# Copying half of the transposed attention probabilities with VectorE instead of ScalarE in the last batch of cross attention

## The chip, the cores and the metric

The kernel runs on one core of one Trainium2 chip. The metric is the device time of one execution in microseconds (us). The engines are PE (TensorE), DVE (VectorE), ACT (ScalarE), POOL (GpSimd) and SP (SyncE, which here only issues DMAs). Each has its own instruction stream in program order, and the streams meet only through semaphores.

## What is computed

The kernel is a whole decoder layer on x of shape (8, 256, 512): a gated delta rule, then cross attention, then a quantised feed-forward. The change touches the cross attention alone:

```python
qh = q.reshape(b, s, 4, 4, 32)            # 4 groups of 4 heads, 32 wide
scores = einsum('bghsd,bgtd->bghst', qh, kh) / sqrt(32)
probs = softmax(scores, axis=-1)
out = einsum('bghst,bgtd->bghsd', probs, vh)
return out.reshape(b, s, 512) @ Wc.T + bc
```

There are 8 batches of 256 query tokens and 256 context tokens. Keys and values are the same context tensor. After the attention, x + out is normalised and quantised for the feed-forward, and the feed-forward's weights are quantised beside the attention.

## The kernel before, in words

The function `attend` holds the stage. A batch's 256 queries are two row tiles u = 0 and 1, and the heads are four groups c = 0 to 3. So a batch is 8 slots (c, u), walked by every engine in the order (0,0), (0,1), (1,0), ... (3,1). The last batch is batch 7, `step(B - 1, True, False, False)`. It projects nothing for a later batch, so PE has less to do in it than in the others.

A tile goes through these steps, each by one engine:

- PE `scores` (L1805) writes the scores of 4 heads into two PSUM banks, `ps_s[u][0]` and `ps_s[u][1]`. It waits for both counters `pt0_done[u]` and `pt1_done[u]` of the tile before in the same banks.
- DVE `maxima` (L2115, two reduces) finds the row maxima of both banks.
- ACT `weigh` (L1989) makes 4 exponentials into `probs[u]`, with the row sums beside.
- PE `turn_probs` (L1813, 8 transposes) writes the probabilities, transposed, back into the same two banks. The first bank holds the half of the 128 first context tokens, the second bank the other half.
- ACT `turned` (L1998, two copies of 128x512 f32) copies the banks to `probs_t[u]` in SBUF, and counts `pt0_done` after the first and `pt1_done` after the second.
- PE `mix` (L1823, 32 matmuls) multiplies the first half by the values after `pt0_done`, then the second half after `pt1_done`.

`turned`, `turn_probs` and `mix` run one slot late: in slot (c, u) they treat `last_tile(b, c, u)`, while `scores`, `maxima` and `weigh` treat the slot's own tile. PE's order in a slot is scores, turn_probs, mix. ACT's order is turned, then weigh. DVE's order is, where they apply: `finish` (L2140) of a tile of the batch before, maxima (L2115), `reciprocals` of the sums (L2122), `weighted` (L2129, multiplies the mixed heads in PSUM by the reciprocals), `mixed` (L2133, the low part of the mixed heads), one chunk of weight quantisation (`chunk`, L2195 to L2224), and a piece of the token quantisation of the batch before (`token_variance` L2145 to L2149, `token_norms` L2154, `token_scales` L2162 to L2175, `token_rounds` L2182). POOL does its own parts of these chunks and tokens (L2325 to L2367).

After the groups of a tile are done, PE `spread` (L1834) lays the reciprocals out, ACT copies them (`r_chan`, L2005), DVE `weighted` uses them, ACT `mixed` makes the high part (L2010), DVE `mixed` the low part, and PE `combine` (L1847 to L1849, 12 matmuls) is the output projection, whose result DVE `finish` adds to the residual. In batch 7, `spread` of tile 0 stands in slot (3,1) and `spread` of tile 1 after the slots. For batch 6, `combine` stands in slots (0,1) and (1,0) of batch 7, behind `mix`. At its first group `mix` waits for `mlo_done`, the count of L2133.

Behind the slots of batch 7 comes a tail: PE transposes the quantised weights in 24 pieces (`turn`, L1935), with the two combines of batch 7 among them, and ACT (L2072) and DVE (L2293) copy them out. The feed-forward starts when that block has ended on all engines.

SP's order of transfers is fixed by hand too. It stores chunks and tokens when POOL has finished them.

Of the kernel before, what the change touches and what calls it, by code (L numbers as in the profile page):

```python
# [12 lines left out]
ACT = mybir.ActivationFunctionType  # L13
# [3 lines left out]
B, T, D = 8, 256, 512  # L17
# [1433 lines left out]
def attend(nc, ident, neg_half, carried, x, ctx_in, out_t, Wc, bc, w_gate, w_up, w_down, x2_dram, xq_dram, wq_dram):  # L1451
# [10 lines left out]
    HEADS, GROUPS, HD = 16, 4, 32  # L1462
# [11 lines left out]
    with ExitStack() as st:  # L1474
        def sb(name, shape, dt):
            return st.enter_context(nc.sbuf_tensor(name, shape, dt))
# [4 lines left out]
        def two(name):  # L1481
            return [sem(f"{name}{u}") for u in U]
# [26 lines left out]
        probs_t = [sb(f"probs_t{u}", [P, 2, PER, P], F32) for u in U]  # L1509
# [29 lines left out]
        ps_s = [[st.enter_context(nc.psum_tensor(f"ps_s{u}{i}", [P, 2 * T], F32)) for i in range(2)] for u in U]  # L1539
# [15 lines left out]
        pt_ps, pt0_done, pt1_done, pv_ps = two("pt_ps"), two("pt0_done"), two("pt1_done"), two("pv_ps")  # L1555
# [33 lines left out]
        def last_tile(b, c, u):  # L1589

            return (b, c, 0) if u else (b, c - 1, 1) if c else (b - 1, GROUPS - 1, 1)
# [3 lines left out]
        with nc.Block() as block:  # L1595
# [355 lines left out]
            def _(act):  # L1951
# [42 lines left out]
                def turned(b, c, u):  # L1994
                    act.wait_ge(pt_ps[u], GROUPS * b + c + 1)
                    act.wait_ge(pv_ps[u], GROUPS * b + c)
                    for k, done in enumerate((pt0_done, pt1_done)):
                        act.activation(probs_t[u][:, k, :, :].rearrange("p j s -> p (j s)"), ps_s[u][k][:, :],  # L1998
                                       ACT.Copy).then_inc(done[u], 1)

                def spread(b, u):

# [81 lines left out]
            def _(dve):  # L2084
                def split(b, u, e):
                    dve.wait_ge(o_hi_done[e], 2 * b + u + 1)
                    dve.tensor_tensor(o_lo[e], o_raw[e], o_hi[e].bitcast(F32),
                                      ALU.subtract).then_inc(o_lo_done[e], 1)

                def residual(b, u):  # L2090

                    dve.wait_ge(y_ps[u], b + 1)
                    dve.wait_ge(x_dma[u], 16 * (b + 1))
                    dve.wait_ge(x1b_done[u], b)
                    dve.tensor_tensor(x1[u][:, :], x_in[u][:, :], ps_y[:, :], ALU.add).then_inc(x1_done[u], 1)

                def variance(b, u):
                    dve.wait_ge(x1_done[u], b + 1)
                    dve.bn_stats(stats[u][:, :], x1[u][:, :])
                    dve.drain()  # L2100
                    dve.bn_aggr(moments[u][:, :], stats[u][:, :]).then_inc(stat[u], 1)
                    dve.wait_ge(stat[u], b + 1)
                    dve.tensor_scalar(var_eps[u][:, :], moments[u][:, 1:2], LN_EPS, None, ALU.add).then_inc(var_done[u], 1)

                def layernorm(b, u):
                    dve.wait_ge(rstd_done[u], b + 1)
                    dve.wait_ge(t_ps[u], b)
                    dve.tensor_scalar(xn[u][:, :], x1[u][:, :], moments[u][:, 0:1], rstd[u][:, 0:1], ALU.subtract,
                                      ALU.mult).then_inc(xn_done[u], 1)

                def maxima(b, c, u):
                    dve.wait_ge(s_ps[u], GROUPS * b + c + 1)
                    dve.wait_ge(exp_done[u], GROUPS * b + c)
                    for i in range(2):
                        last = dve.tensor_reduce(neg_max[u][:, 2 * i:2 * i + 2],  # L2115
                                                 ps_s[u][i][:, :].rearrange("p (j t) -> p j t", j=2), AX_X, ALU.max, negate=True)
                    last.then_inc(max_done[u], 1)

                def reciprocals(b, u):
                    dve.wait_ge(exp_done[u], GROUPS * (b + 1))  # L2120
                    dve.wait_ge(spread_ps[u], b)
                    dve.reciprocal(r_sums[u][:, :], sums[u][:, :]).then_inc(rs_done[u], 1)  # L2122

                def weighted(b, u):

                    dve.wait_ge(pv_ps[u], GROUPS * (b + 1))
                    dve.wait_ge(spread_done[u], b + 1)
                    mixed_heads = ps_v[u][:, :, :].rearrange("p k t -> p (k t)")
                    dve.tensor_tensor(mixed_heads, mixed_heads, r_chan[u], ALU.mult).then_inc(weighted_done[u], 1)  # L2129

                def mixed(b, u):
                    dve.wait_ge(mhi_done[u], b + 1)
                    dve.tensor_tensor(mix_lo[u][:, :, :], ps_v[u][:, :, :], mix_hi[u][:, :, :].bitcast(F32),  # L2133
                                      ALU.subtract).then_inc(mlo_done[u], 1)

                def finish(b, u):
                    dve.wait_ge(c_ps[u], b + 1)
                    dve.wait_ge(x1b_done[u], b + 1)
                    dve.wait_ge(x2_dma[u], 16 * b)
                    dve.tensor_tensor(x2[u][:, :], ps_t[:, :], x1b[u][:, :], ALU.add).then_inc(x2_done[u], 1)  # L2140

                def token_variance(b, u):

                    dve.wait_ge(x2_done[u], b + 1)
                    dve.bn_stats(q_stats[u][:, :], x2[u][:, :])  # L2145
                    dve.drain()
                    dve.bn_aggr(q_moments[u][:, :], q_stats[u][:, :])
                    dve.drain()
                    dve.tensor_scalar(q_var[u][:, :], q_moments[u][:, 1:2], LN_EPS, None, ALU.add).then_inc(q_var_done[u], 1)  # L2149
# [76 lines left out]
                def step(b, before, after, further):  # L2226
                    for c in range(GROUPS):
                        for u in U:
                            if before and (c, u) in ((1, 0), (1, 1)):
                                finish(b - 1, u)  # L2230
                            if after and (c, u) in ((1, 1), (3, 0)):
                                residual(b + 1, 1 - u)
                            maxima(b, c, u)
                            if before and (c, u) == (0, 0):
                                reciprocals(b - 1, 1)
                            if (c, u) == (GROUPS - 1, 1):
                                reciprocals(b, 0)
                            if before and c == 0:
                                weighted(b - 1, u)
                            if before and (c, u) in ((0, 1), (1, 0)):  # L2240
                                mixed(b - 1, c)
                            if after and (c, u) in ((1, 0), (1, 1)):
                                split(b + 1, 1, u)
                            if after and (c, u) == (3, 1):
                                layernorm(b + 1, 1)
                            if further and (c, u) in ((2, 1), (3, 1)):
                                split(b + 2, 0, c - 2)
                            if after and (c, u) in ((1, 1), (3, 0)):
                                variance(b + 1, 1 - u)
                            if (c, u) not in ((1, 1), (2, 1)):  # L2250
                                chunk(b, (0, 1, 2, None, 3, None, 4, 5)[2 * c + u])
                            if after and (c, u) == (2, 0):
                                layernorm(b + 1, 0)
                            if before:
                                if (c, u) == (1, 1):
                                    for tile in U:
                                        token_variance(b - 1, tile)
                                if (c, u) == (2, 0):
                                    token_norms(b - 1)
                                if (c, u) == (2, 1):  # L2260
                                    token_scales(b - 1)
                                if (c, u) == (3, 0):
                                    token_rounds(b - 1)
# [22 lines left out]
                    step(b, True, True, True)  # L2286
                step(B - 2, True, True, False)
                step(B - 1, True, False, False)
                reciprocals(B - 1, 1)
                def weights_turned(t):  # L2290
                    dve.wait_ge(turned_ps, t + 1)
                    place, bank = turned_places(t)
                    dve.tensor_copy(place, bank).then_inc(turned_dve, 1)  # L2293
# [421 lines left out]
```

## Time and profile before

| | us |
|---|---|
| median of 3 runs | 2134.35 |
| lowest and highest of them | 2132.12, 2138.12 |
| the profiled execution's own time | 2132.07 |
| its span, first to last instruction | 2130.4 |
| 1850 to 1905, the slots of batch 7 | 55 |
| 1905 to 1928, the tail of the stage | 23 |

Over the whole span PE is busy for 2001.5 us, DVE for 1710.0, ACT for 1500.8 and POOL for 701.6. These shares are means over three stages with different limits. Start times in the trace count from the start of the span. Records of neighbouring instructions on one engine overlap a little, so what an instruction costs its engine is the distance from its start to the next start, not its own length.

### The profile page before, as it was taken

What the parts mean: (1) busy time and instruction counts of PE and PEld (TensorE: products, weight loads), DVE (VectorE), ACT (ScalarE), POOL (GpSimd) and SP (SyncE); (2) the same over time, 40 slices, a digit from 0 to 9 for tenths busy, and PEclk for the clock granted to TensorE, in tenths of its full rate; (3) what the DMA queues carried; (4) which work ended last, traced back from release to release, by engine and by line L of the source; (5) the groups of instructions that cost most, each with busy time, mean ns of one, the idle gap of its engine ahead of it and who ended that gap; (6) DMA issues with size and microseconds to landing.
All of it is one profiled execution on the core that took longest, in us unless ns stands there. A gap on an engine that the chain in (4) does not pass through costs nothing. (4 is left out here: it accounts for less than half of the span.)

```text
span 2130.4 us, 54757 instructions
## 1 busy us (share of the span) xinstructions
PE 2001.5 (94%) x19285; PEld 1459.5 (69%) x19308; DVE 1710.0 (80%) x3957; ACT 1500.8 (70%) x4249; POOL 701.6 (33%) x601
## 2 busy tenths in 40 slices
PE   6799999999999999999999999969999999878998
PEld 3577777777777777777777777756666666554454
DVE  8687878878877877887887888854789998878997
ACT  2678878878888887887878888844666666654343
POOL 6411121121112112211211121121677777772332
PEclk8899999999999999999999999969999999999999
DMA  3000000000000100100000011114333333242111
GB/s 106 21 20 25 26 20 20 30 10 30 30 10 20 40 10 10 50 10 10 30 30 10 30 35 35 40 50 129 102 110 114 108 102 103 83 160 64 50 62 45
DMA packets 119589, 105.88 MB, mean 50 GB/s; under 512 B 12096, under 2 KB 94016, under 8 KB 119488
## 3 DMA queue, kind: packets, MB, share of 16 engines
q1 hardware_dynamic: 119488, 104.77, 15.9%
q8 instruction: 35, 0.57, 0.1%
q14 instruction: 66, 0.54, 0.1%
HBM read 70.66 MB, written 34.08 MB: 49 GB/s over the span
## 5 line engine op out<-in xcount | busy, mean ns | idle before, releaser
L771 PE MATMUL proj<-xn_hi,w_lo 128*128 x744 | 350.6, 471 | 0.0
L773 PE MATMUL proj<-xn_hi,w_hi 128*128 x744 | 293.8, 395 | 0.0
L772 PE MATMUL proj<-xn_lo,w_hi 128*128 x744 | 292.5, 393 | 0.0
L1177 DVE SCALAR_TENSOR_TENSOR qkv<-conv_in,taps,qkv 128x512 f32<-128x512 f32 x372 | 269.4, 745 | 0.0
L1424 POOL TENSOR_TENSOR o_scale<-o_var,neg_half 128x4 f32<-128x4 f32 x66 | 66.5, 1024 | 526.6 <-DVE o_var L1207 526.5
L1440 POOL TENSOR_TENSOR k_len<-sumsq,pos_half 128x4 f32<-128x4 f32 x31 | 45.4, 1464 | 556.3 <-DVE sumsq L1365 556.3
L1305 DVE TENSOR_TENSOR i_less_r<-bank_c,join_mask 128x256 f16<-128x256 f32 x320 | 120.7, 418 | 94.5 <-PE bank_c L834 93.8
L1087 ACT ACTIVATE inv<-bank_b 128x256 f16<-128x256 f32 x320 | 108.1, 382 | 87.6 <-PE bank_b L855 84.1
L773 PEld LDWEIGHTS proj<-xn_hi,w_hi 128*128 128x128 f32 x744 | 139.9, 188 | 32.6
L1998 ACT ACTIVATE probs_t<-ps_s 128x512 f32<-128x512 f32 x128 | 69.6, 596 | 130.4 <-PE ps_s L1813 130.4
L1032 ACT ACTIVATE g_mask<-mask_ge,g_cols 128x128 fp32r<-128x128 f32 x512 | 153.3, 408 | 8.3 <-DVE g_cols L1397 8.3
L771 PEld LDWEIGHTS proj<-xn_hi,w_lo 128*128 128x128 f32 x744 | 139.8, 188 | 22.8
L772 PEld LDWEIGHTS proj<-xn_lo,w_hi 128*128 128x128 f32 x744 | 141.0, 190 | 7.8
L1989 ACT ACTIVATE probs<-ps_s,neg_max 128x256 f32<-128x256 f32 x256 | 117.9, 484 | 5.0 <-DVE neg_max L2115 4.9
L1336 DVE TENSOR_TENSOR v_r<-v,bank_b 128x256 fp32r<-128x256 f32 x128 | 53.9, 421 | 81.6 <-PE bank_b L882 80.0
L1767 PE MATMUL ps_y<-xn_hi,w_lo 128*128 128x512 f32 x256 | 108.0, 422 | 7.8 <-DVEq L2266 4.5
L2581 ACT ACTIVATE g_silu<-ps_g 128x512 f32<-128x512 f32 x64 | 38.2, 597 | 108.7 <-PE ps_u L2532 108.7
L855 PEld LDWEIGHTS bank_b<-i_less_r,inv_t 64*64 64x64 f16 x2560 | 68.6, 108 | 59.9 <-issue 59.9
L2663 POOL TENSOR_TENSOR i_q<-i,i_scale 128x1024 bf16<-128x1024 fp8e4 x32 | 61.1, 1909 | 135.7 <-DVE i L2634 117.3
L2115 DVE TENSOR_REDUCE neg_max<-ps_s 128x2 f32<-128x512 f32 x128 | 81.6, 679 | 27.2 <-PE ps_s L1805 26.5
L855 PE MATMUL bank_b<-i_less_r,inv_t 64*64 64x64 f16 x2560 | 94.8, 196 | 7.4 <-DVE i_less_r L1305 6.3
L860 PE MATMUL bank_a<-inv_t,i_less_r 64*64 64x64 f16 x2560 | 92.6, 194 | 0.0
(326 smaller groups left out, 5766.2 us busy)
## 6 DMA issues: line engine op xcount, KB each, us to landing
out_t<-o_out SPq DMA_DIRECT2D x66, 256.0 KB, 2.0
w_hi<-out_t SPq DMA_DIRECT2D x32, 512.0 KB, 5.5
w_raw<-in_L_attn_W_qkv_dram SPq DMA_DIRECT2D x32, 256.0 KB, 2.8
wq_dram<-wq_q SPq DMA_DIRECT2D x48, 128.0 KB, 2.0
x_sb<-in_x_dram SPq DMA_DIRECT2D x16, 256.0 KB, 2.7
w_raw<-in_L_attn_W_z_dram SPq DMA_DIRECT2D x16, 256.0 KB, 2.7
w_raw<-in_L_attn_W_out_dram SPq DMA_DIRECT2D x16, 256.0 KB, 2.7
x_in<-in_x_dram SPq DMA_DIRECT2D x16, 256.0 KB, 5.8
```

The costliest lines, as they stand in the source:

```text
L771: pe.matmul(out, w_lo[:, k, cols], sh.xn_hi[:, k, tok], start=(k == 0), stop=False)
L772: pe.matmul(out, w_hi[:, k, cols], sh.xn_lo[:, k, tok], start=False, stop=False)
L773: product = pe.matmul(out, w_hi[:, k, cols], sh.xn_hi[:, k, tok], start=False, stop=(k == KT - 1))
L855: last = pe.matmul(folded(bank_b[s])[rows, hb, :], inv_t[s][rows, hb, :], i_less_r[s][rows, hb, :], start=True, stop=True)
L860: last = pe.matmul(folded(bank_a[s])[rows, hb, :], i_less_r[s][rows, hb, :], inv_t[s][rows, hb, :], start=True, stop=True)
L1032: last = act.activation(g_mask[s][:, i, hb, :], sh.mask_ge[:, :], ACT.Copy, scale=g_cols[:, s, 4 * i + hb:4 * i + hb + 1])
L1087: act.activation(inv[s][:, :, :], folded(bank_b[s]), ACT.Copy).then_inc(t_done[s], 1)
L1177: dve.scalar_tensor_tensor(out=out, in0=conv_in[:, j, :, k:k + T], scalar=taps[:, j, k:k + 1], in1=out, op0=ALU.mult, op1=ALU.add).then_in ...
L1305: dve.tensor_tensor(i_less_r[s][:, :, :], folded(bank_c[s]), bcast(sh.join_mask[:, l + 1, :], 1, 4), ALU.mult).then_inc(r_done[s], 1)
L1767: pe.matmul(ps_y[:, :], o_lo[e][:, g, :], out_weight(wo_hi, k), start=begin, stop=False)
L1989: last = act.activation(probs[u][:, j, :], ps_s[u][j // 2][:, T * (j % 2):T * (j % 2) + T], ACT.Exp, bias=neg_max[u][:, j:j + 1], accum_ou ...
L2115: last = dve.tensor_reduce(neg_max[u][:, 2 * i:2 * i + 2], ps_s[u][i][:, :].rearrange("p (j t) -> p j t", j=2), AX_X, ALU.max, negate=True)
```

## The change

In batch 7 only, ACT's `turned` keeps the first of its two copies, and the second one, from `ps_s[u][1]` to the second half of `probs_t[u]`, becomes a `tensor_copy` on DVE. The tile carried over from batch 6 is still copied by ACT alone, because the call with b = 6 keeps both copies. DVE's copy stands directly behind `maxima` in the 7 slots from (0,1) on, and once more after the last slot, ahead of `reciprocals(B - 1, 1)`. It waits for the same two counters as ACT's and counts the same `pt1_done`.

```diff
@@ act @@
                     for k, done in enumerate((pt0_done, pt1_done)):
-                        act.activation(probs_t[u][:, k, :, :].rearrange("p j s -> p (j s)"), ps_s[u][k][:, :],
-                                       ACT.Copy).then_inc(done[u], 1)
+                        if k == 0 or not (isinstance(b, int) and b == B - 1):
+                            act.activation(probs_t[u][:, k, :, :].rearrange("p j s -> p (j s)"), ps_s[u][k][:, :],
+                                           ACT.Copy).then_inc(done[u], 1)
@@ dve @@
+                def turned(b, c, u):
+
+                    dve.wait_ge(pt_ps[u], GROUPS * b + c + 1)
+                    dve.wait_ge(pv_ps[u], GROUPS * b + c)
+                    dve.tensor_copy(probs_t[u][:, 1, :, :].rearrange("p j s -> p (j s)"), ps_s[u][1][:, :]
+                                    ).then_inc(pt1_done[u], 1)
@@ dve, step @@
                             maxima(b, c, u)
+                            if not after and c + u:
+                                turned(*last_tile(b, c, u))
                             if before and (c, u) == (0, 0):
                                 reciprocals(b - 1, 1)
@@ dve, after the steps @@
                 step(B - 1, True, False, False)
+                turned(B - 1, GROUPS - 1, 1)
                 reciprocals(B - 1, 1)
```

## Rows read from the trace of the kernel before

**Rows 1.** Stretches: length, busy PE, PEld, DVE, ACT, POOL, clock, DMA, GB/s.

```profile
1879.00:1896.00 17.00, 12.07 (x113) 5.89 (x112) 16.46 (x40) 12.17 (x42) 14.77 (x15) 1.00 1.03 325
```

**Rows 2.** Timeline of ACT, one slot: start us, us, instruction, idle before and releaser.

```profile
1887.27 1.08 ACT L1998 ACTIVATE probs_t<-ps_s 128x512 f32<-128x512 f32 x2 [1.18 <-PE ps_s L1813]
1888.24 0.48 ACT L1989 ACTIVATE probs<-ps_s,neg_max 128x256 f32<-128x256 f32 x1
...
1889.94 0.23 ACT L1989 ACTIVATION_READ_ACCUMULATOR probs<-ps_s,neg_max 128x1 f32 x1
1891.36 1.08 ACT L1998 ACTIVATE probs_t<-ps_s 128x512 f32<-128x512 f32 x2 [1.19 <-PE ps_s L1813]
```

**Rows 3.** Timeline of PE, the same slot.

```profile
1890.23 1.09 PE L1813 MATMUL ps_s<-ident,probs 128*128 128x128 f32 x8 [0.34 <-ACT probs L1989]
1892.01 0.92 PE L1823 MATMUL ps_v<-probs_t,ctx_v 128*32 128x128 f32 x16 [0.69 <-ACT probs_t L1998]
```

**Rows 4.** Timeline of DVE, first slots of batch 7.

```profile
1862.19 1.22 DVE L2115 TENSOR_REDUCE neg_max<-ps_s 128x2 f32<-128x512 f32 x2
1863.32 0.69 DVE L2129 TENSOR_TENSOR ps_v<-ps_v,r_chan 128x512 f32<-128x512 f32 x1
1863.92 0.68 DVE L2133 TENSOR_TENSOR mix_lo<-ps_v,mix_hi 128x512 fp32r<-128x512 f32 x1
```

**Rows 5.** Timeline of PE, the same slots: what stands behind mix.

```profile
1865.72 0.64 PE L1847 MATMUL ps_c<-wc_hi,mix_lo 128*128 128x512 f32 x1 [0.42 <-ACT k_blocks L1979]
1873.34 0.64 PE L1823 MATMUL ps_v<-probs_t,ctx_v 128*32 128x128 f32 x16 [0.97 <-DVE mix_lo L2133]
```

**Rows 6.** Timeline of DVE, the later slots of batch 7.

```profile
1878.08 1.29 DVE L2115 TENSOR_REDUCE neg_max<-ps_s 128x2 f32<-128x512 f32 x2 [0.38 <-PE ps_s L1805]
...
1884.14 0.43 DVE L2210 TENSOR_SCALAR wq_step<-wq_y 128x512 int32<-128x512 int32 x1
1884.49 0.17 DVE L2216 TENSOR_SCALAR wq_scale<-wq_pow 128x16 f32<-128x16 f32 x1
...
1885.11 1.64 DVE L2154 TENSOR_SCALAR xm<-x,q_moments,q_rstd 128x512 f32<-128x512 f32 x2
1886.67 1.28 DVE L2115 TENSOR_REDUCE neg_max<-ps_s 128x2 f32<-128x512 f32 x2
...
1889.29 1.11 DVE L2171 TENSOR_SCALAR x_scale<-x_pow 128x16 f32<-128x16 f32 x2
...
1895.44 1.27 DVE L2115 TENSOR_REDUCE neg_max<-ps_s 128x2 f32<-128x512 f32 x2
1896.64 0.23 DVE L2122 RECIPROCAL r_sums<-sums 128x16 f32<-128x16 f32 x1
```

**Rows 7.** Timeline of PE, the end of batch 7's slots.

```profile
1896.93 1.08 PE L1834 MATMUL ps_s<-ident,r_sums 128*32 128x128 f32 x32 [1.53 <-DVE r_sums L2122]
1900.55 1.09 PE L1813 MATMUL ps_s<-ident,probs 128*128 128x128 f32 x8 [2.10 <-ACT probs L1989]
1902.42 1.08 PE L1834 MATMUL ps_s<-ident,r_sums 128*32 128x128 f32 x32 [0.78 <-ACT probs_t L1998]
1905.42 0.50 PE L1847 MATMUL ps_c<-wc_hi,mix_lo 128*128 128x512 f32 x1 [0.48 <-DVE mix_lo L2133]
```

**Rows 8.** Timeline of DVE and of ACT, the tail.

```profile
1904.68 0.69 DVE L2133 TENSOR_TENSOR mix_lo<-ps_v,mix_hi 128x512 fp32r<-128x512 f32 x1 [3.01 <-ACT mix_hi L2010]
1926.38 1.02 ACT L2072 ACTIVATE down_t<-ps_s 128x1024 bf16<-128x1024 bf16 x1
```

**Rows 9.** Timeline of PE and stretches of 1 us: the clock around a wait.

```profile
1864.66 0.64 PE L1823 MATMUL ps_v<-probs_t,ctx_v 128*32 128x128 f32 x16 [2.46 <-DVE mix_lo L2133]
1868.72 0.63 PE L1848 MATMUL ps_c<-wc_lo,mix_hi 128*128 128x512 f32 x1
1875.65 0.39 PE L1848 MATMUL ps_c<-wc_lo,mix_hi 128*128 128x512 f32 x1
1866.00:1867.00 1.00, 1.00 (x3) 0.73 (x3) 1.00 (x2) 1.00 (x7) 0.95 (x1) 0.50 0.00 0
```

## The prediction

> **What bounds the kernel now.** I read the stretches first, because the shares of the whole span mix three stages. In 1879 to 1896, four slots of batch 7, the reader should compare the engines: DVE is busy for 16.46 of 17 us, ACT for 12.17, PE for 12.07 [rows 1]. DVE has hardly any time left, and the change gives it work.
>
> Then the timelines of ACT and PE, which show the loop that the change wants to shorten. ACT starts its two copies at 1887.27, its exponentials 0.97 later, and the next copies at 1891.36: a period of 4.09 us [rows 2]. Between them lies PE: the exponentials end at 1890.17, the transposes run from 1890.23 for 1.09, and ACT copies 0.04 after their end [rows 2, 3]. So the loop is copies 0.97, exponentials 1.95, transposes 1.09 and some 0.1 of signals. All of it is serial, and one ACT copy less would take half of 0.97, so 0.49, off a period.
>
> Then DVE, which runs beside that loop. The maxima of slot (2,1) start at 1886.67 and end 1.28 later, at 1887.95 [rows 6]. ACT's exponentials, which wait for them, start at 1888.24 [rows 2]. DVE's lead is thus 0.29 us. From the maxima of (1,1) at 1878.08 to those of (3,1) at 1895.44 it needs 17.36 us for four slots, 4.34 per slot, which is more than the loop's 4.09 [rows 6, 2]. The two keep step only because DVE entered with a lead. At the end DVE bounds already: PE waits 1.53 us for the reciprocals before spread at 1896.93 [rows 7], and DVE's reciprocals stand 1.20 behind the start of the maxima, in DVE's own order [rows 6].
>
> **The change, part by part.** Seven copies leave ACT within the slots and one behind them, 8 × 0.49 = 3.9 us of ACT time. On the path this is worth something only where maxima are ready earlier than ACT, and the lead of 0.29 says they are not.
>
> Eight copies arrive on DVE. The trace has no DVE copy of 512 f32 from PSUM. The nearest rows are L2129 and L2133, which read 512 f32 of PSUM beside an SBUF operand: 0.69 long and 0.60 from start to start [rows 4]. The lower bound is a one-source operation from SBUF to SBUF, L2210, 0.35 from start to start [rows 6]. The upper bound is an operation that another engine seems to hold up, as L2171, two tiny operations in 1.11 us [rows 6]: I take 1.0 a copy. I take 0.60, the row that also reads PSUM. The Trainium skill (VectorE: DVE Perf Modes, Why PSUM operands drop a tier) says that an f32 operand in PSUM leaves VectorE without its doubled rate, since PSUM has one read port for it. By that the 0.35 can't be reached and the sum stays at its middle value; no row here shows this copy itself.
>
> The copies stand on DVE's own path, so I walk them in its order.
> - Tile (0,0), in slot (0,1), behind the maxima at 1862.19. It delays L2133 of batch 6 by 0.60, and with it mix and combine. But combine waited 0.42 more for ACT's k_blocks [rows 4, 5], and ACT is now earlier. On the path: 0.60 − 0.42 = 0.18.
> - Tile (0,1), in slot (1,0): it delays the second L2133, for which PE waited 0.97 before mix at 1873.34 [rows 5]. Nothing covers it: 0.60. Sum 0.78, carried by combine and finish to the maxima of (1,1).
> - Tiles (1,0), (1,1), (2,0), (2,1): between the maxima of (1,1) and of (3,1) DVE hardly idles, so 4 × 0.60 = 2.40. Sum 3.18.
> - Tile (3,0): it stands between the maxima of (3,1) and the reciprocals of tile 0, for which PE waits [rows 6, 7]: 0.60. Sum 3.78.
> - Tile (3,1), behind the last slot. Before, PE waited 0.78 from the transposes' end to spread at 1902.42, for ACT's first copy [rows 7]. Now DVE copies (0.04 to start, 0.60), then makes the reciprocals (0.2), some 0.9 after the transposes: 0.13 more. Sum 3.9.
>
> The new waits: each DVE copy waits for the transposes of the tile before, and the rest of DVE's slot stands behind it. By the walk the transposes are done by then. In slot (2,0), say, they end at about 1883.8 and the maxima at 1884.4. PE's mix waits for the copy, and scores of the next slot stand behind mix. PE has idle time for that while DVE is late. SP and POOL are not passed by anything that moves; POOL's work follows DVE's signals and shifts with it. ACT's own copy and exponentials wait for nothing new.
>
> What of the 3.9 comes back in the tail? PE takes combine of tile 0 when L2133 at 1904.68 is done [rows 7, 8], and behind it come finish, token quantisation and the transposes of weights, in program order to ACT's last copy at 1926.38 [rows 8]. No transfer there has a fixed time of its own. So the whole of it arrives at the end of the stage, and the feed-forward starts as much later.
>
> The sum is made against the profiled execution: 2132.07 us (span 2130.4) and 3.9 give 2136.0. The median of the runs shown is 2.3 above that execution, so I give the forecast against the median: 2134.35 + 3.9 = 2138.3. With s as the spacing of a copy the sum is (s − 0.42) + 6s + 0.13, the bracket not below zero. It is 2.2 at 0.35 and 6.7 at 1.0.
>
> **The rivals.**
> A. The loop gains. If DVE had room, every copy off ACT would shorten a period by 0.49, and 7 or 8 would give 3.4 to 3.9: about 2130.7. For it speaks the serial loop of [rows 2, 3]. Against it: 4.34 of DVE work against a loop of 4.09. It decides if DVE's slot falls under 3.5 us with its copy in it.
> B. The holds swallow it. L2154 takes 1.64 for two and L2171 1.11 in these slots, for tiny or doubled-rate work, so I take part of it for waits for GpSimd [rows 6]. A DVE that comes 0.6 later may find GpSimd done. I estimate 1.3 us of such time between 1878 and 1896, so the sum would be 2.6: 2137.0. For it: POOL's instructions don't move by as much as DVE's. Against: POOL starts each chunk on DVE's signal, so most of the pattern travels with it.
> C. Slower by more, through the clock. After PE had idled 2.46 before mix at 1864.66, the granted clock was 0.50, the level of 1.2 GHz, in 1866 to 1867, and the matmuls of combine took 0.63; at full clock they take 0.39 [rows 9]. A wait of 2.10 at 1900.55 had no such end [rows 7]. By my walk the wait before spread grows from 1.53 to about 2.6, with a second one of 2.1 behind it. If the clock falls and a combine of batch 7 runs at the lower level, that costs 12 × 0.24 = 2.9, and some 0.9 on a set of transposes: 3.9 + 3.8 = 7.7, 2142.1. It decides from a fall that still holds at the combine, some 6 us after the long wait. That is against it: the fall in batch 7 was over within 4 us (0.63 at 1868.72, 0.39 at 1875.65) [rows 9]. The Trainium skill (TensorE: Matmul & The Clock Gate, HAM oscillation) says that waits between groups of matmuls bring the clock down, and the trace agrees with its 0.50; by that rule alone the change would cost the 7.7.
>
> **How the numbers follow.** Chances: forecast 0.60, A 0.08, B 0.17, C 0.15. 0.3% of this kernel is 6.4 us, about what a measurement can tell from no change. The forecast, A and B all lie within it, so this change is most likely lost in the measurement, with a small real loss. The runs shown differ by 6 us, so the median may lie 2 or 3 off. The range goes from 2134.35 − 0.3 (between A and the low end of the forecast) less 2.5, 2131.5, to C with 2.4 of the runs' spread, 2144.5. Faster by over 0.3%: only A with a lucky median, 0.02. Slower by over 0.3%: most of C, and the forecast's upper bound of 6.7 with a median above it, 0.13. Within: 0.85.
>
> **What would show it.** In the changed trace: a DVE copy with ps_s, 8 times, 0.68 long and 0.60 from start to start; L1998 120 times, not 128. The period of ACT in 1879 to 1896 grows from 4.09 to near 4.9, and ACT's exponentials wait for DVE's neg_max, where they waited for nothing. The maxima of (3,1) start 3.2 later, counted from those of (0,1), spread of tile 0 some 3.8 and the last L2072 some 3.9. The granted clock stays 1.00 from 1896 on. I am wrong if ACT's period shrinks, if the DVE copy waits for the transposes, or if the tail takes back the delay.

## The result, and the profile after

The changed kernel takes 2139.53 us in the median (2137.09 to 2142.60, 21 runs), the kernel before 2134.25 in the same comparison. The ratio is 1.0025 with a 95% interval of 1.0020 to 1.0031, so the change costs 5.3 us (4.3 to 6.6). The forecast was +3.9, 2138.3 in a range of 2131.5 to 2144.5. It is a real loss, though under the 6.4 us that I had called telling.

The start of batch 7 differs between executions of one kernel by some microseconds, through what comes before it. So all traces are laid on one mark here, the start of the maxima of slot (0,1): 1862.19 in the trace of before [rows 4], 1860.34 in that after. The table gives starts after that mark, in us.

| start of | before | after | shift | forecast |
|---|---|---|---|---|
| maxima (1,0) | 9.21 | 9.33 | +0.12 | +0.18 |
| maxima (1,1) | 15.89 | 16.61 | +0.72 | +0.78 |
| maxima (2,0) | 19.63 | 20.62 | +0.99 | +1.38 |
| maxima (2,1) | 24.48 | 26.00 | +1.52 | +1.98 |
| maxima (3,0) | 28.42 | 30.63 | +2.21 | +2.58 |
| maxima (3,1) | 33.25 | 36.60 | +3.35 | +3.18 |
| PE spread, tile 0 | 34.74 | 38.97 | +4.23 | +3.78 |
| PE spread, tile 1 | 40.23 | 44.62 | +4.39 | +3.91 |
| DVE L2133, low part of tile 0 | 42.49 | 47.74 | +5.25 | +3.91 |
| ACT's last copy of the tail | 64.19 | 69.42 | +5.23 | +3.91 |

In the changed file DVE's copy is L2124, ACT's L1999, the maxima L2116, the reciprocals L2130. The copy itself, in a query by line and by stretch (columns as in [rows 1]):

```profile
L2124 DVE COPY probs_t<-ps_s x8: 673/682/691, 1861.5 to 1904.1; 128x512 f32<-128x512 f32 x8
L1999 ACT ACTIVATE probs_t<-ps_s x120: 591/597/602, 1479.7 to 1904.1; 128x512 f32<-128x512 f32 x120
1877.00:1894.00 17.00, 12.20 (x104) 6.52 (x107) 15.77 (x36) 8.61 (x31) 13.62 (x13) 0.82 1.00 321
```

The copy has the size taken, 0.68 long. ACT is busy for 8.61 us in these 17 instead of the 12.17 of [rows 1], and nobody gains by it. DVE's timeline of the changed kernel, around its copies:

```profile
1876.95 1.29 DVE L2116 TENSOR_REDUCE neg_max<-ps_s 128x2 f32<-128x512 f32 x2 [0.38 <-PE ps_s L1805]
1878.16 0.68 DVE L2124 COPY probs_t<-ps_s 128x512 f32<-128x512 f32 x1
1878.76 0.68 DVE L2153 BATCH_NORM_STATS2 q_stats<-x 128x6 f32<-128x512 f32 x1
...
1886.34 1.27 DVE L2116 TENSOR_REDUCE neg_max<-ps_s 128x2 f32<-128x512 f32 x2
1887.54 0.67 DVE L2124 COPY probs_t<-ps_s 128x512 f32<-128x512 f32 x1
...
1890.97 1.29 DVE L2116 TENSOR_REDUCE neg_max<-ps_s 128x2 f32<-128x512 f32 x2 [0.33 <-PE ps_s L1805]
1892.86 0.69 DVE L2124 COPY probs_t<-ps_s 128x512 f32<-128x512 f32 x1 [0.60 <-PE ps_s L1813]
```

From 1878.16 to 1878.76 is 0.60, as forecast. In slot (3,0) the reader sees what the forecast excluded: DVE waits, 0.33 for the scores and 0.60 for the transposes. Why PE is late there stands in PE's timeline and in stretches of 1 us:

```profile
1886.10 0.43 PE L1823 MATMUL ps_v<-probs_t,ctx_v 128*32 128x128 f32 x8 [0.69 <-ACT probs_t L1999]
1888.26 0.66 PE L1823 MATMUL ps_v<-probs_t,ctx_v 128*32 128x128 f32 x8 [1.74 <-DVE probs_t L2124]
1888.85 2.08 PE L1805 MATMUL ps_s<-k_blocks,q_t 64*128 64x512 f32 x4
1890.86 1.97 PE L1813 MATMUL ps_s<-ident,probs 128*128 128x128 f32 x8
...
1904.96 1.93 PE L1834 MATMUL ps_s<-ident,r_sums 128*32 128x128 f32 x32 [0.94 <-DVE r_sums L2130]
```

```profile
1887.00:1888.00 1.00, 0.00 (x0) 0.00 (x0) 1.00 (x3) 0.35 (x1) 0.92 (x2) 0.93 1.08 369
1888.00:1889.00 1.00, 0.74 (x10) 0.35 (x10) 1.00 (x3) 1.00 (x6) 0.92 (x2) 0.50 1.10 370
1897.00:1898.00 1.00, 1.00 (x7) 1.00 (x6) 1.00 (x3) 0.00 (x0) 1.00 (x1) 0.50 0.51 174
1905.00:1906.00 1.00, 1.00 (x20) 0.93 (x24) 0.50 (x1) 0.00 (x0) 0.94 (x1) 0.50 0.00 0
```

PE had waited 0.69 for ACT's half and then 1.74 for DVE's. Within this second wait the granted clock falls to 0.50, the level of 1.2 GHz, and it stays there for ten microseconds. The transposes take 1.97 instead of 1.09 [rows 3]. It falls again at the last spread, which takes 1.93 instead of 1.08 [rows 7]. And it falls a third time at the start of the feed-forward, whose first output addition starts 29.14 after ACT's last copy, not 27.45. After the fall of [rows 9] the kernel before has the clock at 1.00 through the slots, the tail and the start of the feed-forward.

This is not peculiar to the profiled execution. Each timed one has its mean granted clock on record. The mean of these is 0.9777 over 87 executions of the kernel before, and 0.9747 over 31 of the changed one.

### The profile page after: what moved, and what is told of

Its sections match the earlier page's. It is cut to its first block and busy times, and to the rows that moved or that the text cites. A ratio compares the mean times of both kernels' runs of the same rounds, so it can differ in the third digit from the quotient of the medians.

```text
span 2135.4 us, 54765 instructions
## 1 busy us (share of the span) xinstructions
PE 2002.2 (94%) x19285; PEld 1460.2 (68%) x19308; DVE 1713.8 (80%) x3965; ACT 1496.7 (70%) x4241; POOL 701.4 (33%) x601
## 5 line engine op out<-in xcount | busy, mean ns | idle before, releaser
L1999 ACT ACTIVATE probs_t<-ps_s 128x512 f32<-128x512 f32 x120 | 65.7, 596 | 136.1 <-PE ps_s L1813 136.1
L2116 DVE TENSOR_REDUCE neg_max<-ps_s 128x2 f32<-128x512 f32 x128 | 81.6, 679 | 27.7 <-PE ps_s L1805 26.9
```

The costliest lines, as they stand in the source:

```text
L2116: last = dve.tensor_reduce(neg_max[u][:, 2 * i:2 * i + 2], ps_s[u][i][:, :].rearrange("p (j t) -> p j t", j=2), AX_X, ALU.max, negate=True)
```

## The experiments

Marks and shifts are against the table above. Ratios are of the runs to the runs of the kernel before on the same chip, with a 95% interval. The microseconds behind a ratio are what the ratio makes of the time of the kernel before.

**E1, DVE's burden alone.**

```diff
                             maxima(b, c, u)
+                            if not after and c + u:
+                                dve.tensor_reduce(burden[:, :], by_block(bc_row[:, :]), AX_X, ALU.max)
```

and the same once behind the slots.

> The kernel before, with one reduce of 512 f32 on DVE (0.60 us from start to start) in each of the eight places where the change puts its copy; it waits for nothing, nothing waits for it, and ACT keeps both copies. My theory (DVE's time in the slots is what costs): some +3.2 to +3.9 us, with the maxima of (3,1) some 3 us later, counted from those of (0,1); if the clock falls as it did in the changed kernel, up to +5. Rival (the cost lies in the hand-over, PE waiting for a copy from DVE): within 1 us of the kernel before.

Measured: 2138.79, ratio 1.0021 (1.0012 to 1.0029), +4.5 us. Maxima of (3,1) at 35.83 (+2.58), spread of tile 0 at 37.91 (+3.17). From there on the clock is 0.50 for some 9 us, after a first fall of 3 us in slot (3,0), and ACT's last copy is at 69.54 (+5.35). DVE's timeline:

```profile
1899.08 1.28 DVE L2116 TENSOR_REDUCE neg_max<-ps_s 128x2 f32<-128x512 f32 x2
1900.28 0.67 DVE L2236 TENSOR_REDUCE burden<-bc_row 128x16 f32<-128x512 f32 x1
1900.87 0.24 DVE L2123 RECIPROCAL r_sums<-sums 128x16 f32<-128x16 f32 x1
```

An instruction that touches nobody costs as much as the change within the intervals (2.6 to 6.2 us against 4.3 to 6.6), and the clock falls three times here too, though not at the same places. The loss starts with DVE's time, and no hand-over is needed to explain it.

The eleven timed executions stand at two values: six between 2137.84 and 2138.79, with mean granted clocks of 0.976 to 0.978, and five between 2140.34 and 2140.53, with 0.974 to 0.976. The profiled one is of the second group. So the falls of this trace may be missing in part from the first group. There is no trace of an execution of that group.

**E2, ACT's relief alone.** The kernel leaves ACT's second copy out, and only counts.

```diff
+                        if k == 0 or not (isinstance(b, int) and b == B - 1):
                             act.activation(probs_t[u][:, k, :, :].rearrange("p j s -> p (j s)"), ps_s[u][k][:, :],
                                            ACT.Copy).then_inc(done[u], 1)
+                        else:
+                            act.sem_inc(done[u], 1)
```

> The kernel before, with ACT's second copy of each tile of batch 7 left out (the second half of the probabilities stays as it was in SBUF; ACT only counts). My theory (DVE bounds the slots): -0.4 us, from the k_blocks that combine waits for in slot (0,1), and hardly more; the period of ACT stays near 4.1 to 4.3. Rival (ACT's loop bounds, and taking a copy off it is worth 0.49 a slot): -3.4 us.

Measured: 2135.89, ratio 1.0008 (1.0000 to 1.0017), +1.7 us. The expected −0.4 is there up to spread of tile 0: the maxima of (1,0) are at 8.76 (−0.45), those of (3,1) at 32.82 (−0.43). Then:

```profile
1897.55 1.94 PE L1834 MATMUL ps_s<-ident,r_sums 128*32 128x128 f32 x32 [1.99 <-DVE r_sums L2125]
```

PE waits 1.99 where it waited 1.53 [rows 7], the clock falls, and ACT's last copy is at 65.15 (+0.96). With work left out the trace is slower, and the timing is no faster. The gain of the loop does not exist while DVE bounds; rival A is out for this kernel.

**E3, the changed kernel with PE kept busy.**

```diff
+                MIX_FILL, SPREAD_FILL, TURN_FILL = {(2, 0): 6, (2, 1): 4}, 6, 6
+                def filler(n):
+                    pe.wait_ge(x1_done[1], B)
+                    for _ in range(n):
+                        pe.matmul(ps_y[:, :], wc_hi[:, 0, 0:P], wc_hi[:, 0, :], start=True, stop=True)
...
                     for k in range(2):
+                        if k and isinstance(b, int) and b == B - 1 and (c, u) in MIX_FILL:
+                            filler(MIX_FILL[(c, u)])
```

and ahead of the spread of tile 0 and of the last transposes.

> The changed kernel, with idle-time matmuls on PE whose result nobody reads (6 in slot (2,1) and 4 in slot (3,0) between the halves of mix, 6 ahead of spread of tile 0, 6 ahead of the last transposes), so that PE does not rest while DVE is late. Theory (some 2 us of the change's 5.3 are the lower clock in 1888 to 1898 and 1905 to 1909): the clock stays 1.00 from slot (2,0) on, and the time is +3.0 to +3.6 against the kernel before. Rival (the clock costs nothing, it is DVE's time alone): still +5, or more by the matmuls.

Measured: 2136.84, ratio 1.0011 (1.0002 to 1.0020), +2.4 us. Stretches and PE's timeline:

```profile
1890.00:1901.00 11.00, 9.49 (x66) 5.46 (x64) 11.00 (x26) 5.06 (x18) 8.36 (x8) 1.00 1.08 347
1901.00:1911.00 10.00, 7.65 (x130) 6.11 (x131) 6.64 (x14) 4.46 (x13) 9.13 (x8) 1.00 0.16 51
1889.94 1.66 PE L1798 MATMUL ps_y<-wc_hi 128*128 128x512 f32 x6
1891.75 0.43 PE L1831 MATMUL ps_v<-probs_t,ctx_v 128*32 128x128 f32 x8 [0.15 <-DVE probs_t L2135]
```

The clock stays 1.00, DVE has 11.00 of 11, and the marks are: maxima of (3,0) 30.27 (+1.85), of (3,1) 35.49 (+2.24), spreads 37.57 (+2.83) and 43.23 (+3.00), ACT's last copy 67.19 (+3.00), first output addition 27.44 after it. So in the traces the copies cost 3.0 and the clock 2.2 up to the tail's end, with 1.7 more behind it. The timing splits the same way: 2.4 of the 5.3 are left (0.4 to 4.3). That the added matmuls cost nothing of their own is not shown for the six and four between the halves of mix; for those at the other two places see E7.

**E4, two tiles only.** ACT copies tiles (0,0) to (2,1) whole, DVE takes the second halves of (3,0) and (3,1).

```diff
-                        if k == 0 or not (isinstance(b, int) and b == B - 1):
+                        if k == 0 or not (isinstance(b, int) and b == B - 1 and (c, u) in ((3, 0), (3, 1))):
...
-                            if not after and c + u:
+                            if not after and (c, u) == (3, 1):
```

> The change for the tiles (3,0) and (3,1) alone, the other six are copied by ACT as before. Theory (each DVE copy on DVE's path costs its 0.60): 0.60 for tile (3,0) and 0.13 for (3,1), +0.7 us, and with a lower clock at the last spread, as in the changed kernel, up to +1.6. Rival (the copies in the middle slots are harmless, and the last two make the loss): +3 or more.

Measured: 2136.74, ratio 1.0009 (1.0001 to 1.0018), +1.9 us. The reciprocals of tile 0 start at 35.06 instead of 34.45: +0.61 for one copy on the path. Then PE, having waited 2.13, spreads at the lower clock:

```profile
1899.76 1.94 PE L1834 MATMUL ps_s<-ident,r_sums 128*32 128x128 f32 x32 [2.13 <-DVE r_sums L2130]
```

ACT's last copy is at 66.67 (+2.48), more than the 1.6 I allowed. So one copy of 0.61 on the path, and a last one, make a loss of over 2 in the trace. The interval of the timing (0.2 to 3.8 us) does not rule out the rival that the middle tiles are free. The marks do: in E3, at full clock, the maxima of (3,1) are 2.24 late before either of the last two copies can count.

**E5 and E6, less work on DVE.** In both kernels most DVE operations of the weight chunks 2 to 5 in batch 7 and of the tokens of batch 6 treat `W` = 64 columns instead of 512. One of them:

```diff
-                        dve.tensor_scalar(y[:, :], y[:, :], 6.0, -6.0, ALU.min, ALU.max).then_inc(wq_steps, 1)
+                        dve.tensor_scalar(y[:, :W], y[:, :W], 6.0, -6.0, ALU.min, ALU.max).then_inc(wq_steps, 1)
```

> The kernel before with less work on DVE: in batch 7's weight chunks 2 to 5 and in the token quantisation of batch 6 most operations treat 64 of 512 columns (so those parts of the result are left out). It is the base for the next run. Theory: ACT's period is still 4.09 (the loop), spread of tile 0 starts some 0.8 us earlier, 33.9 instead of 34.7 after the maxima of (0,1).

> The changed kernel with the same narrow operations. Theory (rival A of the prediction holds as soon as DVE has room): ACT's period falls from 4.09 to near 3.6, and spread of tile 0 starts some 0.9 us before that of the run just described, at about 33.0 after the maxima of (0,1), though slots (0,1) and (1,0) still cost 0.7. Rival (a copy on DVE is slow to hand over, whatever its load): no period under 4.0, and spread later than in the kernel it is compared with.

Measured: 2135.48, ratio 0.9999 (0.9990 to 1.0009), and 2134.33, ratio 1.0001 (0.9992 to 1.0010). In E5 ACT's periods are 4.09 and spread of tile 0 is at 34.04, as expected. In E6 the periods are 3.60, 3.88, 4.29 and 3.93, and spread is at 34.42: later, not earlier. The expectation failed, and DVE's timeline of E6 shows why: it still has no gap, because narrow operations remain and some of them are long.

```profile
1889.20 0.68 DVE L2124 COPY probs_t<-ps_s 128x512 f32<-128x512 f32 x1
1889.80 0.33 DVE L2172 TENSOR_REDUCE x_max<-xm 128x2 f32<-128x64 f32 x2
1890.05 0.66 DVE L2176 TENSOR_SCALAR x_pow<-x_max 128x16 int32<-128x16 int32 x2
1890.67 1.11 DVE L2181 TENSOR_SCALAR x_scale<-x_pow 128x16 f32<-128x16 f32 x2
```

So the pair did not test what it was made for, and E9 and E10 repeat it.

E5 shows one thing more. PE's timeline and stretches of 1 us, at its last transposes:

```profile
1902.24 1.91 PE L1813 MATMUL ps_s<-ident,probs 128*128 128x128 f32 x8 [2.10 <-ACT probs L1989]
1901.59:1902.59 1.00, 0.35 (x2) 0.35 (x3) 0.37 (x2) 0.60 (x4) 1.00 (x2) 0.88 0.47 151
1902.59:1903.59 1.00, 1.00 (x7) 1.00 (x6) 0.47 (x1) 0.00 (x0) 1.00 (x2) 0.50 0.57 184
```

PE had waited 0.78 before the spread of tile 0, where the kernel before waits 1.53, and then 2.10 as there [rows 7]. It stood still for less, and the clock fell all the same. ACT's last copy is at 65.14 (+0.95), though the spread was 0.70 early. In E9 the same two waits end in the same fall.

**E7, matmuls that nobody reads, in the kernel before:** 5 ahead of spread of tile 0, 6 ahead of the last transposes (`{}, 5, 6` in the constants of E3).

> The kernel before, with matmuls nobody reads on PE ahead of spread of tile 0 (5) and ahead of the last transposes (6), in waits that are there. Theory (the clock falls in many executions of the kernel before too, only not in the profiled one, which is 2 us under the median): -1 to -2.5 us. Rival (the kernel before keeps its clock there in nearly all executions): 0, or up to +0.5 by the matmuls.

Measured: 2134.34, ratio 0.9997 (0.9988 to 1.0006), all marks within 0.03 of before. The rival was right: the kernel before keeps its clock there by itself, and the added matmuls cost nothing that can be measured.

**E8, E7 with token_rounds moved** and 2 matmuls ahead of spread instead of 5.

```diff
-                                if (c, u) == (3, 0):
+                                if (c, u) == (3, 0) and after:
                                     token_rounds(b - 1)
...
                     weighted(B - 1, u)
+                    if u == 0:
+                        token_rounds(B - 2)
                     mixed(B - 1, u)
```

> The run before this one, with 2 matmuls instead of 5 ahead of spread, and with DVE's token_rounds of batch 6 (1.5 us in slot (3,0)) moved behind the slots, where DVE waits 3.0 us. Theory (DVE bounds the last slots, so taking work off it is worth time until ACT's loop bounds): another -0.8 us, maxima of (3,1) 1.5 us earlier. Rival (GpSimd, whose token work moves behind with it, delays the last weights): no gain or a loss.

Measured: 2132.76, ratio 0.9993 (0.9984 to 1.0002), not told from 1. Maxima of (3,1) come at 31.85 (−1.40), spread of tile 0 at 34.00 (−0.74), L2133's counterpart at 41.74 (−0.75): DVE did bound, and the loop takes over after 0.74. But ACT's last copy is at 64.32 (+0.13). The gain is given back in the tail:

```profile
1905.46 1.16 DVE L2221 TENSOR_SCALAR wq_step<-wq_y 128x512 int32<-128x512 int32 x1
1905.22 1.11 POOL L2380 TENSOR_TENSOR wq_q<-wq_t,wq_scale 128x512 bf16<-128x512 f32 x1
```

In the kernel before this DVE operation takes 0.43 in the tail. Here GpSimd, whose work moved behind as well, is still running beside it, and its next step (L2371) starts 46.63 after the mark instead of 46.47. That GpSimd is what lengthens the operation is read from these rows, not tested.

**E9 and E10, real room on DVE.** In both kernels the whole token quantisation of batch 6, on DVE and GpSimd, stands behind the slots.

```diff
-                            if before:
+                            if before and after:
                                 if (c, u) == (1, 1):
                                     for tile in U:
                                         token_variance(b - 1, tile)
```

and the same for token_rstd, scale_tokens and quantise_tokens.

> The kernel before, with the whole token quantisation of batch 6 (on DVE and GpSimd) moved out of batch 7's slots, behind them. DVE then has 1.2 to 3.3 us of work a slot. It is the base for the next run. Theory: ACT's period stays 4.09 in all slots from (1,1) on, since its loop bounds, and spread of tile 0 starts 34.0 after the maxima of (0,1). Total: slower by several us, by the token work in the tail.

> The changed kernel with the same move. Theory (rival A of the prediction holds where DVE has room for its copy): ACT's period is 3.6 in every slot from (1,1) to (3,0), and spread of tile 0 starts at 33.0 or earlier after the maxima of (0,1), 1 us before the run it is compared with. Rival (the copy's place behind maxima and ahead of mix makes a loop of its own): periods of 3.9 or more, no gain.

Measured: 2147.81, ratio 1.0058 (1.0039 to 1.0078), and 2147.33, ratio 1.0059 (1.0042 to 1.0076). Both pay for the tokens in the tail, so only the slots count here. ACT's timelines, first E9's, then E10's:

```profile
1883.38 1.09 ACT L1998 ACTIVATE probs_t<-ps_s 128x512 f32<-128x512 f32 x2 [1.19 <-PE ps_s L1813]
1887.47 1.09 ACT L1998 ACTIVATE probs_t<-ps_s 128x512 f32<-128x512 f32 x2 [1.18 <-PE ps_s L1813]
```

```profile
1881.64 0.60 ACT L1999 ACTIVATE probs_t<-ps_s 128x512 f32<-128x512 f32 x1 [1.18 <-PE ps_s L1813]
1885.24 0.60 ACT L1999 ACTIVATE probs_t<-ps_s 128x512 f32<-128x512 f32 x1 [1.18 <-PE ps_s L1813]
1888.84 0.60 ACT L1999 ACTIVATE probs_t<-ps_s 128x512 f32<-128x512 f32 x1 [1.18 <-PE ps_s L1813]
```

4.09 against 3.60, in every slot from (1,1) on: the loop that rival A described is real, and the half copy is worth exactly its 0.49 as soon as DVE has room. Spread of tile 0 is at 34.04 against 31.99, but 1.06 of this lies before the maxima of (1,0): in E10 the mark itself comes 7.44 after the maxima of (0,0), not 6.14. The totals of the two, with 4 runs each, are not told apart.

**E11 and E12, both kernels unchanged, profiled again.**

> The kernel before, unchanged, profiled once more. Theory (the profiled execution of before, 2 us under its median, had luck with the clock at the end of batch 7): this one shows a lower clock somewhere from spread of tile 0 to the first combine, and its last ACT copy stands 1 to 2.5 us later after the maxima of (0,1) than 64.2. Rival: 64.2 again, no lower clock there.

> The changed kernel, unchanged, profiled once more. Theory (the long wait before the second half of mix in slot (2,1) is in the order of the work and sends the clock down each time): lower clock again from about slot (2,1) on, and the last ACT copy 68.5 to 70 after the maxima of (0,1). Rival (the fall in the first profile was chance): full clock, and 67.2.

Measured: 2133.78, ratio 0.9998 (0.9988 to 1.0008), and 2139.98, ratio 1.0026 (1.0015 to 1.0037). The marks repeat to 0.02: ACT's last copy at 64.18 and 69.43, against 64.19 and 69.42. The kernel before has no lower clock there, so my idea of a lucky profile was wrong. The changed kernel has it at the same places, from 27 to 37, from 44 to 48 and from 71 to 76 after the mark.

## Why the prediction was right, and where it was off

**What bounds.** Right. DVE had no time left in the slots, and its work is the path (E1, E8). The point at which it turns is shown from both sides: at 4.34 of DVE work a slot the copy loses, with the tokens out it gains 0.49 (E9, E10).

**The cost of a copy.** 0.60 was taken and 0.60 measured, in the changed kernel and as +0.61 in E4. The lower bound of 0.35 did not come. This agrees with the Trainium skill (VectorE: DVE Perf Modes, Why PSUM operands drop a tier), which has no doubled rate for an f32 operand in PSUM.

**The steps in slots (0,1) and (1,0).** 0.18 and 0.78 forecast, 0.12 and 0.72 measured.

**The four copies between the maxima of (1,1) and (3,1).** This term was mis-sized: 2.40 forecast, 2.24 − 0.72 = 1.52 measured at full clock (E3). Copies push DVE into time that it had lost anyway. That is rival B's mechanism, with 0.9 of its 1.3. DVE's timelines, of the kernel before and of E3, show where it lies:

```profile
1880.69 0.69 DVE L2145 BATCH_NORM_STATS2 q_stats<-x 128x6 f32<-128x512 f32 x1 [0.24 <-issue]
1889.06 0.29 DVE L2166 TENSOR_SCALAR x_pow<-x_max 128x16 int32<-128x16 int32 x2
1892.34 0.64 DVE L2202 TENSOR_SCALAR wq_y<-wq_y 128x512 f32<-128x512 f32 x1
1892.90 0.16 DVE L2205 TENSOR_SCALAR wq_pow<-wq_max 128x16 int32<-128x16 int32 x1
```

```profile
1883.33 0.68 DVE L2164 BATCH_NORM_STATS2 q_stats<-x 128x6 f32<-128x512 f32 x1
1892.81 0.84 DVE L2185 TENSOR_SCALAR x_pow<-x_max 128x16 int32<-128x16 int32 x2
1893.81 0.36 DVE L2194 RECIPROCAL x_inv<-x_scale 128x16 f32<-128x16 f32 x2
1896.42 0.42 DVE L2221 TENSOR_SCALAR wq_y<-wq_y 128x512 f32<-128x512 f32 x1
```

The pause between the halves of token_variance is 0.32 shorter. x_pow and x_scale together take 1.00 instead of 1.26. The two wq_y operations take 0.33 each instead of 0.41 and 0.56. That adds up to 0.9. What held these operations up before is not shown.

**The last two copies.** 0.60 and 0.13 forecast; 0.59 and 0.17 in E3.

**The tail.** Right that it takes nothing back: +3.00 at the last spread is +3.00 at ACT's last copy in E3, and +5.25 at L2133 is +5.23 in the changed kernel.

**The new waits.** Partly wrong. A DVE copy that waits for the transposes was to be a sign of error. At full clock no copy in the slots does (E3). In the changed kernel two do, 0.60 and 0.18, because the transposes run at the lower clock. ACT's period was to grow to near 4.9. In the slots from (1,1) to (3,0) of E3 it is 3.60, 3.88, 5.37 and 4.68, mean 4.38. It shrinks in the first two, where the maxima are still early enough. PE's idle time did not cover the hand-over: PE waits 1.74 for a copy in slot (2,1).

**The clock.** This step failed. The forecast counted nothing for it, had it at 1.00 from 1896 on, and put rival C, a fall behind the long wait at spread that would reach the combines, at 0.15. What happened is a fall already in slot (2,1), within a wait of 1.74, shorter than the 2.10 that the kernel before bears. It costs scores, transposes and spreads, not the combines, 2.2 us up to the tail's end. That PE's standing still is behind it is shown: with matmuls in its waits the clock stays at 1.00 (E3). Which waits lower it is not. Neither the longest wait nor the sum of the waits decides: the clock falls in E5 behind 0.78 and 2.10, and stays in the kernel before behind 1.53 and 2.10. So the rule by which rival C goes, that waits bring the clock down, can't be used here to say when. Rival C had the right mechanism with the wrong place and price. Its 0.24 for a combine is moreover a difference of lengths; from start to start it is 0.43 − 0.23 = 0.20.

So 3.9 against 5.3 is the sum of a term too large by 0.9 and one missing of over 2. That the forecast came so close is luck in this part: the two errors have opposite signs.

Beyond the tail the changed kernel also starts the feed-forward at the lower clock, +1.7 in both its traces. By its traces it should then lose 6.9, and the timing says 5.3 (4.3 to 6.6). The way from the mark to the first output addition is 91.64 and 91.62 in the two traces of the kernel before, 98.56 and 98.49 in those of the changed one, and from there to the end it is 176.5 to 176.6 in all four. The traces of E1, E2 and E4 overshoot their timings too. The mean granted clock of the timed executions goes with the traces: 0.9758 to 0.9767 for E1, E2, E4 and E5, whose traces have late falls, and 0.9775 to 0.9790 for E3, E6, E7 and E8, whose traces have none. Whether the falls are missing from some of the timed executions, or batch 7 starts earlier in them, stays open.

No version here is shown to beat the kernel before. E8 is the nearest, with an interval that holds 1.

## What to carry to other kernels

Before work is moved to relieve an engine, compare the receiver's time per step with the giver's period, in that stage alone: 4.34 against 4.09 gave the sign, and the busy shares of the span (80% and 70%) did not show it. Then ask what PE does while the later engine is late: its added waits can cost as much again through the clock, even where each is shorter than waits that were harmless. When it does was not to be read from the waits beforehand.

## What I had not expected of the hardware

Leaving work out made the kernel no faster: E2 saves 0.43 us up to the first spread, and ends 0.96 later in the trace (ratio 1.0008, 1.0000 to 1.0017), since PE's wait grew from 1.53 to 1.99 and the granted clock went to 0.50. Adding matmuls that nobody reads, 22 of them, made the changed kernel faster: from a ratio of 1.0025 (2139.53) to 1.0011 (2136.84). The falls of the clock were no noise in the changed kernel: two executions, with the mark at 1860.34 and 1863.06, had them within 0.1 of the same places. In E1 the timed executions stand at two values 2.4 us apart. And standing still for less did not save the clock in E5.
